# Cross-attention for 16 batches: layer norm in PSUM, the output bias as a matmul, one batch of queries a step, visits of scores in pairs

## The reference

```python
Q = (query @ Wq.T + bq); K = (key_value @ Wk.T + bk); V = (key_value @ Wv.T + bv)   # 16 heads each
scores = einsum('bhqd,bhkd->bhqk', Q, K) / sqrt(16)
context = einsum('bhqk,bhkd->bhqd', softmax(scores), V)
x = context @ W_o.T + b_o + query
mu = mean(x); var = mean(square(x - mu))                 # over the 256 features
return (x - mu) / sqrt(var + 1e-5) * gamma + beta
```

## Time and profile before

| | us |
|---|---|
| median of three runs | 232.86 |
| range of the runs | 232.59 to 237.04 |
| the profiled execution's own span | 230.5 |

### The profile page before, as it was taken

One profiled execution on the slowest core, in us unless ns is written; L12 is line 12 of the kernel. 1 busy time (PEld: TensorE's weight loads), 2 busy tenths in 40 slices (PEclk: granted clock), 3 DMA queues, 4 the chain that ended last, 5 costly groups with the idle time before them and its releaser, 6 DMA issues.

```text
span 230.5 us, 6883 instructions
## 1 busy us (share of the span) xinstructions
PE 206.8 (90%) x2740; PEld 190.9 (83%) x2740; DVE 181.4 (79%) x378; ACT 172.3 (75%) x313; POOL 182.9 (79%) x163
## 2 busy tenths in 40 slices
PE   0999998899999899989999899989998999997930
PEld 0998797799899789978999699969996899997820
DVE  5699977378778977887888878787878787986494
ACT  4589489678778769795888588958796788887440
POOL 9999454877379958997699769975999499999873
PEclk9999999999999999999999999999999999999995
DMA  6946322345611153115321532143124111121022
GB/s 206 331 73 201 62 53 72 117 124 175 159 50 48 46 148 92 50 51 137 92 57 48 129 66 80 60 119 81 46 68 86 43 48 46 57 87 46 3 94 91
DMA packets 24808, 20.96 MB, mean 91 GB/s; under 512 B 10554, under 2 KB 21953, under 8 KB 24776
## 3 DMA queue, kind: packets, MB, share of 16 engines
q1 hardware_dynamic: 23544, 19.26, 30.1%
q10 hardware_dynamic: 1232, 1.26, 1.8%
HBM read 11.32 MB, written 4.19 MB: 67 GB/s over the span
## 4 chain that ended last, share of the span: by engine, by line
PE 52%; POOL 15%; DVE 12%; issue 10%; ACT 7%; DMA 2%; POOLq 0%; DVEq 0%; ACTq 0%
PE ps_s L348 18%; PE ps_x L348 14%; PE ps_acc L348 13%; POOL p_l L1042 9%; PE ps_d L348 6%; DVE result L905 4%; DVE xT_l L764 4%; ACT p_h L684 3%; POOL result L1050 2%; POOL x_rows L1059 2%; DMA w_raw<-in_wkT 2%; POOL rs_y L1071 2%; PE ps_x L509 1%; ACT ctx_h L691 1%; DVE vrest L796 1%
## 5 line engine op out<-in xcount | busy, mean ns | idle before, releaser
L1042 POOL TENSOR_TENSOR p_l<-p,p_h 128x512 f16<-128x512 f32 x80 | 99.1, 1243 | 34.5 <-ACT p_h L684 34.1
L850 DVE TENSOR_REDUCE maxima<-ps_d 128x4 f32<-128x308 f32 x128 | 58.8, 464 | 23.6 <-PE ps_d L348 23.2
L683 ACT ACTIVATE p<-ps_s 128x512 f32<-128x512 f32 x80 | 47.3, 592 | 21.7 <-PE ps_s L348 21.0
L348 PE MATMUL ps_acc<-vblk,p_h 128*128 128x34 bf16 (+1 forms) x960 | 52.0, 183 | 2.0 <-POOL p_l L1042 2.0
L348 PE MATMUL ps_s<-q_low,kblk 128*128 128x256 f32 x192 | 51.2, 298 | 1.1 <-issue 1.0
L348 PEld LDWEIGHTS ps_acc<-vblk,p_h 128*128 128x128 f16 x960 | 43.2, 96 | 10.3 <-issue 3.2
L348 PE MATMUL ps_acc<-vblk,p_l 128*128 128x34 bf16 (+1 forms) x640 | 48.4, 181 | 0.0
L684 ACT ACTIVATE p_h<-ps_s 128x512 f16<-128x512 f32 x80 | 47.2, 590 | 0.0
L348 PE MATMUL ps_s<-q_lo,kblk 128*128 128x256 f32 x160 | 45.0, 282 | 0.0
L348 PE MATMUL ps_d<-kblk,q_low 128*128 128x308 f32 x128 | 41.4, 327 | 0.2 <-DVE maxima L850 0.2
L348 PEld LDWEIGHTS ps_acc<-vblk,p_l 128*128 128x128 f16 x640 | 38.7, 96 | 0.0
(11 more groups left out here) (90 smaller groups left out, 446.8 us busy)
## 6 DMA issues: line engine op xcount, KB each, us to landing
xT_raw<-in_xT SPq DMA_DIRECT2D x8, 512.0 KB, 4.1
x_rows<-in_x SPq DMA_DIRECT2D x16, 256.0 KB, 2.9
out_dram<-result SPq DMA_DIRECT2D x15, 256.0 KB, 2.2
kblk<-kT SPq DMA_DIRECT2D x64, 38.5 KB, 2.3
c_raw<-in_cT ACTq DMA_DIRECT2D x4, 308.0 KB, 3.8
vblk<-vparts SPq DMA_DIRECT2D x4, 184.1 KB
rows_sb<-in_bias_rows SPq DMA_DIRECT2D x1, 384.0 KB, 7.2
kblk<-kblk SPq DMA_DIRECT2D x3, 96.0 KB, 2.4
```

Of the source, the lines that this page charges most:

```text
L348: return nc.tensor.matmul(o, w, m, start=start, stop=stop, skip_group_check=True)
L683: nc.scalar.activation(p32[:, n % P32SLOTS], ps_s[n % 2][:], ACT.Exp, scale=SCALE)
L850: v_.tensor_reduce(maxima[:, t, h0:h0 + DMAX_HEADS], ps_d[((DMAX + 1) * (s + 1) + j) % 2][:, 0:DMAX_HEADS * SKV] .rearrange("p (h k) -> p ...
L1042: g_.tensor_tensor(p_l[:, n % PSLOTS], p32[:, n % P32SLOTS], p_h[:, n % PSLOTS], ALU.subtract).then_inc(rest16, 1)
```

## The change

- `y` stays in PSUM. The residual is added in place, centring writes it back to PSUM, and a new `finish` on DVE multiplies with the root, adds beta and writes `result` in SBUF; ACT's scaling and POOL's beta are gone. The next `project_out` waits for `finish`. The last batch uses a bank of `ps_s`.
- The output bias is put into `y` by two matmuls in front of the projection: `bias_sel` has two rows of ones, `bias_two` the bias and its rest. POOL's addition is gone.
- In every step up to 13 PE projects the queries of one batch (12 matmuls of 256 columns, one bank). ACT writes them once (two of 256 columns), POOL copies them to `q_high`, DVE makes the rest.
- PE visits scores 0 and 1 in a row, then weighs units 3 and 4; projects; visits 2 and 3, weighs 0 and 1; turns the context; visits 4, weighs 2; turns the maxima; projects out. Maxima 0 and 1 are in visit 0, number 2 is behind the projection, 3 and 4 in visit 2, 5 behind the turned context, 6 and 7 in visit 4.
- `write_maxima` moves behind the last exponentials of the step on ACT; the roots move forward on POOL, behind the third subtraction.

```diff
+        ps_y = [ps_s[0][:].rearrange("p a q -> p (a q)") if b == B - 1 else ps_x[1][:] for b in range(B)]
...
+                    y = ps_y[s - 1]
+                    if 0 in halves:
...
+                        if s < B:
+                            S.wait(pe, result_done, QT, -QT)
+                        for qt in range(QT):
+                            mm(y[:, qt * D:(qt + 1) * D], bias_sel[:], bias_two[:], qt == 0, False)
                     S.wait(pe, ctx_lo, 1, halves[-1] if s == B else 0)
...
+                scores(0, 0, 1)
+                scores(1)
+                weighing(3, 1)
+                weighing(4, 1)
+                if S.project_q:
+                    next_q()
+                if S.maxima:
+                    max_scores(2)
+                scores(2, 3, 4)
+                scores(3)
+                weighing(0, 0)
+                weighing(1, 0)
+                if S.output and s < B:
+                    turn_context(0, 1)
+                if S.maxima:
+                    max_scores(5)
+                scores(4, 6, 7)
+                weighing(2, 0)
+                if S.maxima:
+                    turn_maxima()
+                if S.output and s < B:
+                    project_out(0, 1)
...
+            def batch_query_hi(b):
+
+                cols = slice(b % 2 * SQ, (b % 2 + 1) * SQ)
+                for f in range(HALVES):
+                    ins = nc.scalar.activation(q_low[b // 2 % 2][:, f, cols], ps_x[0][:, f * SQ:(f + 1) * SQ], add,
+                                               bias=bq_sb[:, f:f + 1])
+                ins.then_inc(q_hi, 1)
...
+                def centre():
+
+                    S.wait(dve, var_done, QT, -QT)
+                    for t in range(QT):
+                        y_t = y[:, t * D:(t + 1) * D]
+                        v_.scalar_tensor_tensor(y_t, y_t, meanvar[:, t, 0:1], gamma_sb,
+                                                ALU.subtract, ALU.mult).then_inc(centred, 1)
+
+                def finish():
 
                     o = s % 2
+                    if s == 2:
+                        dve.wait_ge(v_low, V_TASKS)
+                    S.wait(dve, centred, QT, -QT)
+                    S.wait(dve, root_done, 1, -1)
+                    S.wait(dve, st_out[o], 8, -16 - 8 * o)
+                    for t in range(QT):
+                        v_.scalar_tensor_tensor(result[:, o, t], y[:, t * D:(t + 1) * D], rs_y[:, o, t:t + 1], beta_sb,
+                                                ALU.mult, ALU.add).then_inc(result_done, 1)
...
                 when(S.output, (denominators, 0))
                 when(S.maxima, (max_of, 0))
                 when(S.output, (normalize, 0))
                 when(S.maxima, (max_of, 1))
-                when(s == B, (denominators, 1), (normalize, 1))
                 when(S.norm, (residual,))
-                when(s == B, (context_lo_part, 0))
+                when(S.output, (denominators, 1), (normalize, 1))
                 when(S.maxima, (max_of, 2))
...
+                when(S.norm, (statistics,))
                 when(S.maxima, (max_of, 3))
...
+                when(S.norm, (aggregate,))
                 when(S.maxima, (max_of, 4))
...
+                when(S.norm, (centre,))
+                when(S.project_q, (queries,))
+                when(S.maxima, (max_of, 5))
+                when(S.norm, (finish,))
+                when(S.output, (context_lo_part, 0, 1))
                 when(S.maxima, (max_of, 6))
                 when(S.maxima, (max_of, 7))
...
+                def queries_again():
+                    b = s + 2
+                    cols = slice(b % 2 * SQ, (b % 2 + 1) * SQ)
+                    S.wait(pool, q_hi, 1, 3)
+                    g_.tensor_copy(q_high[b // 2 % 2][:, :, cols],
+                                   q_low[b // 2 % 2][:, :, cols].bitcast(F32)).then_inc(q_copied, 1)
```

More of the change, by code:

```diff
@@ L401, in project_q, with project_batch_q @@
                       lambda b, k: (xT_h, xT_l)[b][:, k, :]).then_inc(pe_q, 1)
+            def project_batch_q(half):
+                cols = slice(half * SQ, (half + 1) * SQ)
+                for f in range(HALVES):
+                    ins = three(ps_x[0][:, f * SQ:(f + 1) * SQ], lambda a, k: (wq_h, wq_l)[a][:, k, f * P:(f + 1) * P],
+                                lambda b, k: (xT_h, xT_l)[b][:, k, cols])
+                ins.then_inc(pe_q, 1)
             project_k(0)
@@ new lines, in next_q, with scores, weighing @@
+                    S.wait(pe, ctx_lo, 1, -1)
+                    project_batch_q(s % 2)
+                def scores(u, *tasks):
+                    for n in range(2):
+                        if S.scores:
+                            score_tile(u, n)
+                        if S.maxima and n < len(tasks):
+                            max_scores(tasks[n])
+                def weighing(u, back):
+                    if S.output if back else S.scores:
+                        weigh(u, 0, back)
+                        weigh(u, 1, back)
@@ new lines, in step @@
+                if s == -1:
+                    for u in range(UNITS - 1):
+                        max_scores(2 * u)
+                        max_scores(2 * u + 1)
+                        between[u]()
+                    turn_maxima()
+                    return
+                scores(0, 0, 1)
[6 more added lines that the diff above has]
+                    max_scores(2)
@@ L706, in step @@
                 for u in range(UNITS):
-                    if u == 4 and S.maxima:
-                        write_maxima()
-                    if u == 3 and S.output and s < B and S.project_q:
-                        context_hi_part(0, 1)
                     if S.scores:
@@ L714, in step @@
                         value_mid(V_TASKS - 2 + u)
-                    if u < HALVES and S.project_q:
-                        S.wait(act, pe_q, 1, 3 + u)
+                    if u == 1 and S.project_q:
+                        S.wait(act, pe_q, 1, 3)
                         S.wait(act, pe_s, UNITS, 0)
-                        query_hi(u, (s // 2 + 1) % 2)
-                    if u == (2 if S.project_q else 1) and S.store and s < LAST_STEP:
-                        S.wait(act, root_done, 1, -2)
-                        S.wait(act, centred, QT, -2 * QT)
-                        for t in range(QT):
-                            r = result[:, (s - 3) % 2, t]
-                            nc.scalar.activation(r, r, copy, scale=rs_y[:, (s - 3) % 2, t:t + 1]).then_inc(scaled, 1)
+                        batch_query_hi(s + 2)
                     if s == B and u == 0:
@@ L728, in step @@
                         context_hi_part(1)
-                    if u == 3 and S.output and s < B and not S.project_q:
+                    if u == 3 and S.output and s < B:
                         context_hi_part(0, 1)
@@ L771, in _ @@
             v_.memset(maxima[:], 0.0).then_inc(cleared_m, 1)
+            v_.memset(bias_sel[:].bitcast(F32), 0.0).then_inc(sel_zero, 1)
+            dve.wait_ge(sel_zero, 1)
+            for row in (0, BROWS // 2):
+                v_.memset(bias_sel[row:row + 1].bitcast(F32), 1.0).then_inc(sel_set, 1)
             def weight_lo(n):
@@ L837, in step @@
                 stats, meanvar = stats_all[:, own], meanvar_all[:, own]
-                y_s = x_rows[:, (B - 1) % 2] if last else y[:]
+                y = ps_y[s - 2] if S.norm else None
                 def accumulated(f):
@@ L923, in when @@
                             fn(*args)
-                if last:
+                if s == B:
+                    denominators(0)
+                    normalize(0)
+                    denominators(1)
+                    normalize(1)
                     residual()
-                    dve.wait_ge(y_done, B)
-                    statistics(0)
-                    statistics(1)
-                    dve.wait_ge(stats_done, QT * B)
+                    context_lo_part(0)
+                    statistics()
+                    context_lo_part(1)
                     aggregate()
-                    dve.wait_ge(var_done, QT * B)
-                    centre(0)
-                    centre(1)
-                    dve.wait_ge(centred, QT * B)
-                    dve.wait_ge(root_done, B)
-                    for t in range(QT):
-                        r = result[:, (B - 1) % 2, t]
-                        v_.scalar_tensor_tensor(r, r, rs_y[:, (B - 1) % 2, t:t + 1], beta_sb, ALU.mult, ALU.add).then_inc(finished, 1)
+                    centre()
+                    finish()
                     return
```

173 lines of the change are left out of this document (63 added, 110 removed).

## The result

The changed kernel takes 271.98 us in the median of 4 runs (270.49 to 273.19), the kernel before beside it 234.74 us (232.59 to 237.04): a ratio of 1.1686, interval 1.1608 to 1.1763. It is slower by 17%, where 6.5% was forecast. The direction was right; the time lies 16 us above the range. (Ratios are formed from undisturbed runs alone, so they can differ a little from the quotient of two medians.) The profiled execution has a span of 268.7 us, 38.2 us more than before.

The account below looks back on a forecast made before the run. PE was taken to bound the kernel before, DVE's queue behind maximum 2 the changed one. Span 230.5 us, plus 15.2 (steps 1 to 13) and 1.6 (step 14), less 1.3 and 0.2, gave 245.8, so 248 us; range 236 to 256.

Parts of the forecast that it names:

- the walk: One full step followed from its first score matmul through PE's and DVE's work to the next step: 12.99 us.
- extra cycles for PSUM: Rule for DVE's six operations on y: 62 cycles more each, 0.39 us a step, 251 us in all; the forecast rejected it.
- The wait for `xT_l`: PE's stall at the query projection, behind slow centring on DVE; its removal saves at most 1.3 us per pair of steps.
- The copy on POOL: POOL's new 128x512 copy of the queries, estimated at 1.0 us and hidden at any cost up to 1.3 us.
- the 0.06 us that the forecast had added: Allowance per step, because the same walk gave 23.85 us for two steps of the kernel before against 23.98 measured.
- The operations run without a break: DVE's train behind maximum 2 is continuous, 6.39 us from 4.61 to 11.00 us, making PE wait 1.7 us every step.
- Turning the maxima 0.14 and the output projection with its bias 14 x 0.118 + 0.09: PE's work behind its wait for maxima: 0.14 us and 1.74 us, so the next step starts at 12.93 us.
- PE's clock: Rival: the waits drop PE to its lower clock, 7 to 8 us of matmuls could double, over 270 us; chance 0.03.
- If PE never waited, the loop would gain: PE's own work after the change is 22.5 us per pair of steps, 11.3 us a step, against 23.98 a pair before.
- DVE keeps up: Rival: DVE's train from maximum 2 to 7 under 4.8 us, PE never waits, about 222 us; chance 0.07.

Follow-up runs that it names:

- x2: Changed kernel with statistics, aggregation and centring moved ahead of maximum 2 on DVE, finish ahead of maximum 5, low context last, POOL's roots before its copy: 240.5 us, ratio 1.0317.
- x3: Changed kernel with PE making maxima 2 to 7 earlier, spread over the visits, and DVE's order to fit: steps of 12.35 us, runs of 240.91 and 246.09 us.
- x1: Changed kernel with one swap in DVE's order, the low parts of the queries before the centring: 259.08 us, ratio 1.1114, steps of 13.50 us.
- x4: Changed kernel with the matmul of maximum 7 issued 8 times, filling PE's wait before turning the maxima: 268.29 us, ratio 1.1509.
- x8: Changed kernel with the two bias matmuls ahead of turning the maxima instead of behind: steps of 13.81 us, runs of 259.65 and 263.77 us.
- x5: Changed kernel, same operations, with the orders of PE, DVE, ACT and POOL all rearranged: 229.31 us, ratio 0.9736 to the kernel before, steps of 11.52 us.

## Why the prediction was right, and where it was wrong

**What held.** PE bound the kernel before, and the changed kernel turns this round: DVE's work behind maximum 2 sets the step (x2 shows it with PE's program untouched, and x3 fits). The single terms of the walk were good: maximum 2 on PE 4.27 us into the step (4.25 said), DVE's train starting at 4.61 us as said, the train without its break 6.24 us long (7.19 from 193.75 to its end at 200.94, less 0.95; 6.39 said), the root at 8.8 us (8.7), centring and finish at 485 and 476 ns (470 said). Of the extra cycles for PSUM that the Trainium skill names ("VectorE: DVE Perf Modes", section "The TRN2 errata") no run here shows anything: a pair of centrings takes 0.88 us in PSUM, where the undisturbed pair of before took 0.87 from SBUF. The row that the forecast held against that rule was misread, though: its 674 ns are a mean over two shapes ("+1 forms"). The fifteen subtractions over 128x512 with an input in PSUM alone take 692 ns, those from SBUF alone 670 to 693, so the conclusion stands. The wait for `xT_l` is gone. The copy on POOL cost less than taken:
```profile
194.51 0.61 POOL L1052 CAST q_high<-q_low 128x512 fp32r<-128x512 f32 x1 [0.86 <-ACT q_low L648]
```
That is 0.61 us, inside the bounds of 0.45 and 1.24, and it is hidden as argued.

**What failed, term by term.** The forecast's step is 12.99 us, the undisturbed one 14.13: 1.14 us missing. In the step from 189.14 us turning the maxima starts at 11.86 us instead of 11.05 (0.81), takes 0.33 instead of 0.14 (0.19), the bias 0.43 instead of 0.24 (0.19) and the projection 0.01 more than its share; less the 0.06 us that the forecast had added, that is the 1.14.
- *The sentence "The operations run without a break" was false: 0.81 us.* The break in the train is 0.95 us, and the rest of the train was 0.15 shorter than said. x1 gives 0.63 us of it back. The walk asked of each maximum whether PE would be there before DVE, with PE never waiting before `turn_maxima`. It left out that since the change one bank of `ps_x` holds first the batch's queries and then the turned context. So `turn_context` waits for `q_lo`, and `q_lo` stood behind the centring in DVE's queue. The wait is in the code for all to see, and the forecast's own terms give its length. PE reaches `turn_context` at 4.25 + 0.14 + 1.70 + 1.04 = 7.1 us; DVE has the queries done at 4.61 + 1.16 + 0.67 + 0.15 + 0.79 + 0.78 + 0.08 = 8.2 us. Measured is a wait of 1.05 us. The walk went through DVE's queue and checked what each operation needs, but not through PE's waits a second time with the new times.
- *"Turning the maxima 0.14 and the output projection with its bias 14 x 0.118 + 0.09" was too low: 0.38 us.* It stands behind the wait, on the path. The extra 0.19 us of the turning isn't a restart after standing still: in x4, after a wait of only 0.23 us, turning takes 0.33 us too, and in x8, after 0.79 us, 0.15. It comes with the bias matmuls right behind it. The 0.118 us was of matmuls over 128 rows in a running stream. With the 64-row bias matmuls the spacings are 0.20 us from the second turning to the first of them, 0.22 to the second and 0.21 to the projection. Their place doesn't matter: they are 0.22 to 0.23 us apart also behind a weighing (x8) and behind scores (x5), so being first in the projection isn't the reason. No run has them with 128 rows. x8, which moves them, gains 0.32 us, because ACT's writes then hold the next step.
- *PE's clock*, a rival at 0.03 with a price of over 270 us. It did happen, at a smaller price. In steps 2 to 13 the slow steps are together 5.1 us longer than 12 of 14.13 us, and step 14, at 13.53 us, is 1.5 us longer than in x4 (12.06): 6.6 us of the 38.2. That x4's steps are all alike, though PE works more in them, speaks for PE's idle time as what brings the stretches on; and each of the five begins 1.0 to 1.6 us after the wait at `turn_maxima` has ended (at 171.22 us, for one, and the clock falls at 172.7). It is the second wait that seems to matter: x8, with waits of 1.05 and 0.8 us, has none in steps 2 to 14, and x1, with 0.3 and 1.4, has two. That is read from one trace each and not shown beyond it. The rival's condition was judged by one window at 85% busy and by one stall in two steps. Neither resembles two waits in every step. Its price was the doubling of all matmuls, where only some stretches were slowed.

The whole difference in span: steps 1 to 13, 187.0 - 152.6 = 34.4 us (29.3 undisturbed, 5.1 clock); step 14 3.7 us (1.5 of it clock); step 0, 0.4; the end -0.2, together 38.3 against 38.2 measured. Forecast were 15.2, 1.6, 0 and -1.5. The end did not gain, although its centrings fell as said: one stretch at the lower clock begins 1.2 us ahead of it and reaches 2.2 us into it, another ends it, and x4, which is spared the first of them, ends in 22.0 us instead of 23.0. Of the 22.9 us by which the span missed the forecast, the undisturbed steps 1 to 13 carry 29.3 - 15.2 = 14.1, the clock 6.6, and step 14 (0.6), the end (1.3, most of it clock again) and step 0 (0.4) the rest, to rounding.

**The side that was not taken.** "If PE never waited, the loop would gain" was right and is shown: with 11.5 us a step x5 is 2.6% faster than the kernel before. The rival *DVE keeps up* priced this at 222 us; the best measured is 226.75, the median 229.31. The change's parts are sound; the hand-written order around them, with what it does to the clock, is what costs 17%.

## What to carry to other kernels

Walk a changed schedule twice: once along the queue that becomes the bound, and once more along the other engine with the new times, looking for each buffer that the change makes two users share; a wait there feeds back into the queue. What stands behind a wait on the critical engine, even a small bias matmul, costs its full time, and whatever needs nothing from the wait belongs ahead of it. Moving it gives back only as much as the next waiter allows: here 0.32 of 0.61 us, because another engine's writes, just hidden before, came into view. When an engine that was 90% busy is made to wait in every step, ask what its clock does, and price it with a few slowed stretches, not with all or nothing.

## What the runs showed of the hardware

- PE's granted clock fell to 1.2 GHz for 3.41 us at a time in a loop where PE worked 11.88 of 14.14 us and stood still for 1.05 and 1.21 us (before the last of the five stretches once, for 1.41). It stayed at 2.4 GHz in steps 2 to 14 where only the second wait was filled (x4) or cut from 1.2 to 0.8 us (x8), and fell twice where the first was cut to 0.3 us and the second was 1.4 (x1), each in one profile.
- Two float32 matmuls of 256 columns over 64 rows were 0.22 us apart start to start in three different places (after, x5, x8), against 0.118 over 128 rows in a stream; the turning ahead of them took 0.33 us, and 0.15 where 128-row matmuls followed it.
- DVE operations with PSUM as input cost what undisturbed ones in SBUF cost (a pair over 128x256 0.88 us, and 0.87 before), and POOL's work didn't hold them up: the pair of `finish` took 0.87 us from 198.71 us on, with a subtraction of POOL running since 197.94. The split of x, which has both inputs in SBUF, was held up: 2.14 us in the kernel after, where a subtraction of POOL had begun at 200.77 us. In the kernel before it took 1.21 us, though a like subtraction of POOL began 0.05 us after it; there it was POOL's that took longer, 2.19 us instead of 1.16. At all eleven splits of the two loops the one that began second was the slow one (2.14 us for the split, 1.66 to 2.19 for POOL's). No run changes the order alone.
```profile
200.87 2.14 DVE L763 TENSOR_TENSOR xT_l<-xT_raw,xT_h 128x1024 fp32r<-128x1024 f32 x1
```
```profile
126.34 1.21 DVE L764 TENSOR_TENSOR xT_l<-xT_raw,xT_h 128x1024 fp32r<-128x1024 f32 x1
126.39 2.19 POOL L1042 TENSOR_TENSOR p_l<-p,p_h 128x512 f16<-128x512 f32 x1 [0.25 <-ACT p_h L684]
```
